# A fused four-layer network: cross attention of the last layer in two passes through DRAM, and layer 0 with its turned copies a step earlier

## The chip, the cores and the metric

The kernel runs on one core of a Trainium2 chip. The metric is the device time of one execution in microseconds (us), the median of several runs. The engines are TensorE (PE in the rows), VectorE (DVE), ScalarE (ACT), GpSimd (POOL) and the queue engine SyncE (SP), which issues nearly all DMA transfers. TensorE's clock has two levels, 1.2 and 2.4 GHz; the column PEclk of a stretch is the granted share of the full clock.

## The reference, cut to what matters

Four layers run one after the other on x of 8 entries x 100 tokens x 512: a grouped cross attention (32 heads over 8 key heads, layer 0), an RWKV layer, a plain attention, and layer 3, which has two cross attentions and an MLP. Context has 8 x 361 x 512 values. Layer 3 is (16 heads of 128, queries 100 tokens, keys and values 361 rows and one learned row):

```python
def _cross_attention(q_in, kv_in, wq, bq, wk, bk, wv, bv, wo, bo, bias_k, bias_v):
    qh = (q_in @ wq + bq).reshape(b, q_len, H, K)
    kh = (kv_in @ wk + bk).reshape(b, t, H, K)
    vh = (kv_in @ wv + bv).reshape(b, t, H, K)
    kh = jnp.concatenate([kh, jnp.broadcast_to(bias_k, (b, 1, H, K))], axis=1)
    vh = jnp.concatenate([vh, jnp.broadcast_to(bias_v, (b, 1, H, K))], axis=1)
    logits = jnp.einsum('bqhk,bthk->bhqt', qh, kh) / scale
    weights = jax.nn.softmax(logits, axis=-1)
    ctx = jnp.einsum('bhqt,bthk->bqhk', weights, vh).reshape(b, q_len, H * K)
    return ctx @ wo + bo
...
    h = _layer_norm(x, ln1_scale, ln1_offset)
    x = res + _cross_attention(h, xf_1, wq1, bq1, wk1, bk1, wv1, bv1, wo1, bo1, bias_k1, bias_v1)
    ...
    x = res + _cross_attention(h, xf_2, wq2, bq2, wk2, bk2, wv2, bv2, wo2, bo2, bias_k2, bias_v2)
```

## The kernel before

X stays in SBUF from layer to layer. Each layer opens a scope, in it a block with one program for each engine, ordered by hand and joined by semaphores. Matmuls of layer 3 take each operand as a high and a low part and use three products (low x high, high x low, high x high), the helper `products`.

**Layer 3.** `attention_block` (L2127) starts the first loads, runs the layer norm with its turning (highT, lowT), and calls `cross_attention` (L1469), twice in all. That runs 32 steps: 4 groups of 4 heads, for each the 8 entries. The engines' loops are hardware loops over half groups (4 steps). One step of TensorE (L1884) makes the keys of the entry for the 4 heads (48 matmuls, 362 wide), turns the probabilities of the step before (12 transposes), makes values (36 matmuls, 512 wide) with the attended product of the step before between them, the output product of the step before (12 matmuls, 512 wide), and the scores of this step (12 matmuls, 362 wide). Each fourth step starts with the queries of a half (48 matmuls, 400 wide). ScalarE copies high parts out of the banks (keys L1689, turned probabilities L1664, values L1699, attended L1669 and L1672) and makes the exponentials (L1657); VectorE makes the low parts, maxima and the normalising. POOL splits each loaded context into high and low (L1595, L1597) and each of the four weights of a group (L1610, L1612), each one when TensorE has let go of the buffer. VectorE adds each step's output to X. SP loads contexts and weights ahead.

**Layer 0.** `grouped_attention` (L190) runs 25 tiles for each of the 8 entries. In step n TensorE makes score n in one of RS banks (L562), and turns tile n-LT in one of RT banks (L519); it waits for the copy that frees the bank. VectorE adds the mask and takes the maximum (L476) and turns some copies out; ScalarE's step n is the exponential of tile n (L408) and then the copy of turned tile n-LE (L398).

## Time and profile before

| what | us |
|---|---|
| median of 3 runs (range) | 3397.99 (3397.32 to 3402.0) |
| profiled execution, its time | 3401.78 |
| profiled execution, its span | 3400.0 |
| load and start of layer 0 | 0 to 78 |
| layer 0, attention | 78 to 391 |
| rest of layer 0, layers 1 and 2 | 391 to 1280.6 |
| layer 3, first attention block | 1280.6 to 2247.9 |
| layer 3, second attention block | 2247.9 to 3215.6 |
| MLP and end | 3215.6 to 3400 |

Over the span TensorE is busy 2887.7 us (85%), VectorE 1613.1, ScalarE 980.1 and GpSimd 879.9. A matmul's duration overlaps the next one's, so the time that one costs TensorE is the distance from its start to the next start. A time in brackets at the end of a row is how long the engine stood idle before it, with the instruction that ended it.

### The profile page before, as it was taken

The numbers are of one execution on the slowest core, as the hardware profiler recorded it, in microseconds if no ns is written. First come the engines' busy times: TensorE is split into PE (matmuls) and PEld (weight loads), VectorE is DVE, ScalarE is ACT, GpSimd is POOL, SyncE is SP. The second block draws the span as 40 slices with busy tenths as digits, with TensorE's granted clock in tenths as the row PEclk, the third lists the DMA queues.
The fourth block names the chain that finished last, engine by engine and source line by source line (L and its number), as shares of the span: only waits on it lengthen the run. The fifth ranks groups of instructions, "written<-read, shape, count | busy, mean of one in ns | idle before, by whom it ended". The sixth has DMA issues, their size and how long they took to land. (4 is left out here: it accounts for less than half of the span.)

```text
span 3400.0 us, 42583 instructions
## 1 busy us (share of the span) xinstructions
PE 2887.7 (85%) x14746; PEld 2274.8 (67%) x14746; DVE 1613.1 (47%) x2985; ACT 980.1 (29%) x2236; POOL 879.9 (26%) x465
## 2 busy tenths in 40 slices
PE   5777749766678796998998999959989989989789
PEld 3555324333333465987987988948878879879689
DVE  2444451099952126445445445455454454454453
ACT  1555311100021113333333333333333323323231
POOL 2000022145510005333343342132352343432020
PEclk8888768899989997999999999969999999999889
DMA  4343010310000323111111101011111111100110
GB/s 151 79 94 91 11 61 39 119 37 20 20 0 0 118 72 113 39 39 51 39 51 39 39 30 35 10 70 61 39 55 35 39 56 46 39 17 26 53 50 20
DMA packets 73361, 170.13 MB, mean 50 GB/s; under 512 B 12180, under 2 KB 28972, under 8 KB 72236
## 3 DMA queue, kind: packets, MB, share of 16 engines
q1 hardware_dynamic: 73196, 168.77, 15.6%
q8 instruction: 57, 0.93, 0.1%
q14 instruction: 44, 0.36, 0.0%
q10 hardware_dynamic: 64, 0.07, 0.0%
HBM read 152.52 MB, written 14.65 MB: 49 GB/s over the span
## 5 line engine op out<-in xcount | busy, mean ns | idle before, releaser
L1595 POOL TENSOR_TENSOR ca_ch<-att_craw,ca_nothing 128x1448 fp32r<-128x1448 f32 x64 | 167.1, 2611 | 843.1 <-PE ca_ring L1821 843.0
L1821 PE MATMUL ca_ring<-ca_ch,ca_wl 128*128 128x362 f32 x1024 | 343.0, 335 | 26.1 <-DVE ca_ql L1777 26.1
L1821 PE MATMUL ca_ring<-ca_ch,ca_wh 128*128 128x362 f32 x1024 | 342.1, 334 | 0.0
L1821 PE MATMUL ca_ring<-ca_cl,ca_wh 128*128 128x362 f32 x1024 | 341.6, 334 | 0.0
L1657 ACT ACTIVATE ca_probs<-ca_score,ca_shift 100x362 f32<-100x362 f32 x256 | 140.7, 563 | 335.8 <-DVE ca_shift L1802 335.8
L1784 DVE SCALAR_TENSOR_TENSOR ca_kl<-ca_ring,ca_columns,ca_kh 128x361 fp32r<-128x361 f32 x256 | 145.7, 590 | 171.1 <-ACT ca_kh L1689 171.1
L1821 PEld LDWEIGHTS ca_ring<-ca_ch,ca_wl 128*128 128x128 f32 x1024 | 197.8, 193 | 28.8 <-DVE ca_ql L1777 16.8
L1597 POOL TENSOR_TENSOR ca_cl<-att_craw,ca_ch 128x1448 fp32r<-128x1448 f32 x64 | 215.6, 3369 | 5.0
L1689 ACT ACTIVATE ca_kh<-ca_ring,ca_columns 128x361 fp32r<-128x361 f32 x256 | 143.7, 567 | 254.0 <-PE ca_ring L1821 253.7
L1821 PE MATMUL ca_ring<-ca_wh,ca_cl 128*128 128x512 f32 (+1 forms) x512 | 205.4, 401 | 0.0
L1821 PE MATMUL ca_ring<-ca_wh,ca_ch 128*128 128x512 f32 (+1 forms) x512 | 201.7, 394 | 0.0
L1821 PE MATMUL ca_ring<-ca_wl,ca_ch 128*128 128x512 f32 (+1 forms) x512 | 201.3, 393 | 0.0
L1821 PEld LDWEIGHTS ca_ring<-ca_cl,ca_wh 128*128 128x128 f32 x1024 | 197.9, 193 | 0.0
L1821 PEld LDWEIGHTS ca_ring<-ca_ch,ca_wh 128*128 128x128 f32 x1024 | 197.2, 193 | 0.0
L871 PE MATMUL rec_sum<-rec_seen,l_gather 128*128 128x400 f32 x256 | 122.7, 563 | 85.9 <-POOL rec_seen L885 85.9
L476 DVE CUSTOM_DVE_ANT_0 ga_masked<-ga_score,ga_maskb 128x361 f32<-128x361 f32 x200 | 105.7, 534 | 161.2 <-PE ga_score L562 144.6
L1758 DVE TENSOR_TENSOR ca_mid<-ca_mid,ca_ring 128x200 f32<-128x200 f32 x64 | 23.3, 363 | 326.4 <-ACT ca_mid L1669 326.4
L909 DVE TENSOR_TENSOR_SCAN rec_state<-rec_wb,rec_rank 128x400 f32<-128x400 f32 x128 | 177.7, 1393 | 0.0
L1745 DVE TENSOR_SCALAR ca_probs<-ca_probs,ca_share 100x362 f32<-100x362 f32 x256 | 175.6, 749 | 2.3
L519 PE MATMUL ga_turn<-state_ident,ga_probs 128*128 128x128 f32 x600 | 118.7, 314 | 66.6 <-ACT ga_probs L408 50.8
L885 POOL TENSOR_TENSOR rec_seen<-rec_state,rec_rb 128x400 f32<-128x400 f32 x128 | 138.5, 1085 | 137.4 <-DVE rec_state L909 135.3
L1610 POOL TENSOR_TENSOR ca_wh<-att_raw,ca_nothing 128x2048 fp32r<-128x2048 f32 x24 | 86.5, 3602 | 286.6 <-PE ca_ring L1821 286.6
(355 smaller groups left out, 6797.5 us busy)
## 6 DMA issues: line engine op xcount, KB each, us to landing
att_craw<-in_ctxT SPq DMA_DIRECT2D x64, 724.0 KB
att_raw<-in_L_xattn_wq SPq DMA_DIRECT2D x8, 1024.0 KB
att_raw<-in_L_xattn_wk SPq DMA_DIRECT2D x8, 1024.0 KB
att_raw<-in_L_xattn_wv SPq DMA_DIRECT2D x8, 1024.0 KB
att_raw<-in_L_xattn_wo SPq DMA_DIRECT2D x8, 1024.0 KB
mlp_raw<-in_L_xattn_w_fc SPq DMA_DIRECT2D x4, 2048.0 KB
l_ctx<-in_ctxT SPq DMA_DIRECT2D x8, 724.0 KB
l2a_ctxT<-in_ctxT SPq DMA_DIRECT2D x8, 724.0 KB, 4.8
```

The costliest lines, as they stand in the source:

```text
L476: nc.vector.tensor_tensor_reduce(masked[:, n % RM, :], score[n % RS][:, 0:S], maskb[:, b % 2, lb, :], -1.0, 3.0e38, ALU.add, ALU.min, top[ ...
L519: last = nc.tensor.transpose(turn[n % RT][:, t, :], probs[:, n % RP, t * P:(t + 1) * P], ident[:])
L871: nc.tensor.matmul(sumb[par][:, :, 0:L], gather[:, j, :], seen[j % 4][:].rearrange("p (c l) -> p c l", l=L), start=(j == 0), stop=(j == HD ...
L885: nc.gpsimd.tensor_tensor(seen[j % 4][:], state[j % 4][:], rb[:, par].rearrange("p c l -> p (c l)"), ALU.mult).then_inc(seen_done, 1)
L909: nc.vector.tensor_tensor_scan(state[j % 4][:], wb[:, par].rearrange("p c l -> p (c l)"), rank1[:, j].rearrange("p c l -> p (c l)"), 0.0, ...
L1595: nc.gpsimd.tensor_tensor(flat(ch[:, parity]), flat(craw[:]), nothing[:].broadcast_to([P, CC * SP]), ALU.add).then_inc(ctx_high, 1)
L1597: nc.gpsimd.tensor_tensor(cl[:, parity], craw[:], ch[:, parity].bitcast(F32), ALU.subtract).then_inc(ctx_ready, 1)
L1657: nc.scalar.activation(probs[:, h, :], score[h][0:L, 0:SP], ACT.Exp, bias=shift[:, h:h + 1], scale=scale, accum_out=total[:, h:h + 1]).the ...
L1689: nc.scalar.activation(kh[:, h, 0:S], ring[h][:, 0:S], ACT.Identity, bias=column(1, n, h)).then_inc(high_done, 1 if i or h < G3 - 1 else 1 ...
L1745: nc.vector.tensor_scalar(probs[:, h, :], probs[:, h, :], share[:, h:h + 1], None, ALU.mult).then_inc(probs_ready, 1)
L1784: nc.vector.scalar_tensor_tensor(kl[:, h, 0:S], ring[h][:, 0:S], column(1, n, h), kh[:, h, 0:S].bitcast(F32), ALU.add, ALU.subtract).then_ ...
L1821: last = nc.tensor.matmul(out, a, b, start=(k == 0), stop=(k == count - 1))
```

## The change

**Layer 3** is split in two passes. `projections` (L1469 of the changed kernel) splits all 8 contexts once and keeps them in SBUF, makes all queries (32 units of 12 matmuls, 400 wide) and then all keys (128 units of 12 matmuls, 362 wide), and writes them to DRAM: queries as high and low parts (13.1 MB), keys as whole numbers (23.7 MB); X with the output bias is written there too. `attention` (L1681) reads them back a step ahead. A key comes into `kl`; ScalarE copies its high part to `kh` (`high_key`), POOL subtracts in place (`low_key`). Values are no longer made: the turned probabilities are multiplied with the raw context (`mix`, 36 matmuls, 400 wide), which POOL splits for each step, and each fourth step the value weights (`heads`, 4 x 13 matmuls, 400 wide, with one matmul for the learned row, whose probabilities SP gathers with three small transfers a step, `stack_extra`) and the output weights (`outputs`, 48 matmuls, 400 wide) are applied to half a group. The output is summed turned, in `acc`, and turned back and added to X at the end of the block, after X was read back: X's room serves as the landing place of contexts and weights meanwhile. All loops are unrolled.

**Layer 0**: `RS` 4 to 3, `RT` 2 to 3, one lag of 5 for the turning and its copy, and ScalarE's copy now stands ahead of the exponential in a step. The load of X waits for a small memset.

ScalarE, a middle step of the block, before: four exponentials of a step, then the first key copies out of the banks (probs: probabilities; kh: key's high part).

```order
L1657 ACTIVATE ca1_probs,ca1_total<-ca1_score0,ca1_shift 100x362
L1657 ACTIVATE ca1_probs,ca1_total<-ca1_score1,ca1_shift 100x362
L1657 ACTIVATE ca1_probs,ca1_total<-ca1_score2,ca1_shift 100x362
L1657 ACTIVATE ca1_probs,ca1_total<-ca1_score3,ca1_shift 100x362
L1688 ISA
L1689 ISA
L1689 ACTIVATE ca1_kh<-ca1_ring0,ca1_columns 128x361
L1688 REGISTER_ALU
L1689 ISA
L1689 ACTIVATE ca1_kh<-ca1_ring1,ca1_columns 128x361
```

The same engine after, one whole step n of the attention pass (pp: turned probabilities of n; yh: mixed context of n; probs: of n+2; kh: key of n+3).

```order
L1909 ACTIVATE ca1_pp<-ca1_ring0 128x400
L1909 ACTIVATE ca1_pp<-ca1_ring1 128x400
L1909 ACTIVATE ca1_pp<-ca1_ring2 106x400
L1915 ACTIVATE ca1_yh<-ca1_ring3 128x4x100
L1900 ACTIVATE ca1_probs,ca1_total<-ca1_score0,ca1_shift 100x362
L1915 ACTIVATE ca1_yh<-ca1_ring0 128x4x100
L1900 ACTIVATE ca1_probs,ca1_total<-ca1_score1,ca1_shift 100x362
L1915 ACTIVATE ca1_yh<-ca1_ring1 128x4x100
L1900 ACTIVATE ca1_probs,ca1_total<-ca1_score2,ca1_shift 100x362
L1915 ACTIVATE ca1_yh<-ca1_ring2 128x4x100
L1900 ACTIVATE ca1_probs,ca1_total<-ca1_score3,ca1_shift 100x362
L1894 ACTIVATE ca1_kh<-ca1_kl 128x1448
```

The key copy is now one of 1448 columns, and stands behind the last copy of the mixed context.

POOL in the block, before: two contexts and one weight.

```order
L1595 TENSOR_TENSOR ca1_ch<-att1_craw,ca1_nothing 128x1448
L1597 TENSOR_TENSOR ca1_cl<-att1_craw,ca1_ch 128x1448
L1608 ISA
L1609 ISA x2
L1610 TENSOR_TENSOR ca1_wh<-att1_raw,ca1_nothing 128x2048
L1611 ISA
L1612 TENSOR_TENSOR ca1_wl<-att1_raw,ca1_wh 128x2048
```

POOL after, steps 0 to 2 of the attention pass (kl: a key's low part; xh, xl: a context's parts; wvh, wvl: the value weights' parts; state_X is the landing place).

```order
L1854 TENSOR_TENSOR ca1_kl<-ca1_kl,ca1_kh 128x1448
L1861 TENSOR_TENSOR ca1_xh<-state_X,ca1_nothing 128x1536
L1864 TENSOR_TENSOR ca1_xl<-state_X,ca1_xh 128x1536
L1854 TENSOR_TENSOR ca1_kl<-ca1_kl,ca1_kh 128x1448
L1861 TENSOR_TENSOR ca1_xh<-state_X,ca1_nothing 128x1536
L1864 TENSOR_TENSOR ca1_xl<-state_X,ca1_xh 128x1536
L1870 TENSOR_TENSOR ca1_wvh<-state_X,ca1_nothing 128x2048
L1872 TENSOR_TENSOR ca1_wvl<-state_X,ca1_wvh 128x2048
L1854 TENSOR_TENSOR ca1_kl<-ca1_kl,ca1_kh 128x1448
```

A key's subtraction was added ahead of each context's two, and the weights' stand between.

ScalarE at the start of layer 0's attention, before (ga_turn0, 1: the banks of turned tiles).

```order
L395 ACTIVATE ga_kh<-ga_front,l0_bk 128x362
L408 ACTIVATE ga_probs<-ga_masked,ga_top 128x361 x7
L398 ACTIVATE ga_lturned<-ga_turn0 128x384
L408 ACTIVATE ga_probs<-ga_masked,ga_top 128x361
L398 ACTIVATE ga_turned<-ga_turn1 128x3x128
```

And after:

```order
L395 ACTIVATE ga_kh<-ga_front,l0_bk 128x362
L410 ACTIVATE ga_probs<-ga_masked,ga_top 128x361 x5
L398 ACTIVATE ga_lturned<-ga_turn0 128x384
L410 ACTIVATE ga_probs<-ga_masked,ga_top 128x361
L398 ACTIVATE ga_turned<-ga_turn1 128x3x128
L410 ACTIVATE ga_probs<-ga_masked,ga_top 128x361
L398 ACTIVATE ga_turned<-ga_turn2 128x3x128
```

The first copy stands two exponentials earlier, and copies go through three banks.

The diff, cut:

```diff
-    RS, RM, RP, RT = 4, 6, 6, 2
-    LT, LE = 5, 6
+    RS, RM, RP, RT = 3, 6, 6, 3
+    LAG = 5
...
-            for n in range(total + LE):
+            for n in range(total + LAG):
                 b, i = place(n)
+                if n >= LAG and not by_dve(n - LAG):
+                    keep_turned(act, n - LAG, copy, kept_act)
                 if n < total:
                     act.wait_ge(masked_done, n + 1)
                     if n >= RP:
                         act.wait_ge(turn_full, n - RP + 1)
                     nc.scalar.activation(probs[:, n % RP, 0:S], masked[:, n % RM, :], ACT.Exp, bias=top[:, n % RM:n % RM + 1],
                                          scale=-1.0).then_inc(exp_done, 1)
-                if n >= LE and not by_dve(n - LE):
-                    keep_turned(act, n - LE, copy, kept_act)
...
-                if LT <= n < total + LT:
-                    turn_tile(n - LT)
+                if LAG <= n < total + LAG:
+                    turn_tile(n - LAG)
...
+    BANKS = 8
+    QS, KS = 2, 4
...
+            for k in range(2 * NG3):
+                g, half = k // 2, k % 2
+                sp.wait_ge(query_low, G3 * (k + 1))
+                sp.dma_start(queries[g, :, :, :, half * HALF:(half + 1) * HALF], qstage[:, k % QS].bitcast(F32)).then_inc(
+                    queries_out[k % QS], 16)
+                if k + 2 < B:
+                    load_context(k + 2)
+                if half == 1:
+                    load_weights(g + 2)
+            for n in range(STEPS):
+                sp.wait_ge(kept_act, G3 // 2 * (n + 1))
+                sp.wait_ge(kept_dve, G3 // 2 * (n + 1))
+                sp.wait_ge(learned, n + 1)
+                sp.dma_start(keys[n], kstage[:, n % KS]).then_inc(keys_out[n % KS], 16)
...
+            for b in range(B):
+                split_context(b)
...
+            for g in range(NG3):
+                pe.wait_ge(weight_ready, g + 1)
+                for half in range(2):
+                    rows = slice(half * BH, (half + 1) * BH)
+                    for h in range(G3):
+                        bank_free(u - BANKS)
+                        products(nc, bank[u % BANKS][:, 0:HALF].rearrange("p (b l) -> p b l", l=L), [
+                            (weight(g, h, c), (highT[:, rows, c, :], lowT[:, rows, c, :])) for c in range(CC)]).then_inc(full, 1)
+                        u += 1
+            for n in range(STEPS):
+                g, b = n // B, n % B
+                j = NG3 + g
+                pe.wait_ge(weight_ready, j + 1)
+                if g == 0:
+                    pe.wait_ge(ctx_ready, b + 1)
+                for h in range(G3):
+                    bank_free(u - BANKS)
+                    products(nc, bank[u % BANKS][:, 0:SP], [
+                        (weight(j, h, c), (ch[:, b, c, :], cl[:, b, c, :])) for c in range(CC)]).then_inc(full, 1)
+                    u += 1
...
+        raw, craw = spare[:, 0:CC * W3], spare[:, CC * W3:CC * W3 + 3 * C].rearrange("p (t c) -> p t c", c=C)
+        acc = sc.sb("acc", [P, CC, B * L])
...
+            def load_key(n):
+                if n >= 2:
+                    sp.wait_ge(score_full, G3 * (n - 1))
+                sp.dma_start(kl[:, n % 2], keys[n]).then_inc(k_in[n % 2], 16)
...
+            def load_context(n):
+                sp.wait_ge(x_ready, n)
+                b = n % B
...
+            def stack_extra(n):
+                sp.wait_ge(turn_low, 3 * (n + 1))
...
+                if n + 2 < STEPS:
+                    load_query(n + 2)
+                    load_key(n + 2)
+                if n + 1 < STEPS:
+                    load_context(n + 1)
+                if n % B == 0:
+                    load_differences(n // B)
+                if n % B == 2:
+                    load_outputs(n // B)
+                if n % B == B - 2 and n + 2 < STEPS:
+                    load_values(n // B + 1)
+                stack_extra(n)
...
+            def low_key(n):
+                pool.wait_ge(k_high, n + 1)
+                nc.gpsimd.tensor_tensor(kl[:, n % 2].bitcast(F32R), kl[:, n % 2], kh[:, n % 2].bitcast(F32), ALU.subtract).then_inc(k_ready, 1)
...
+            low_key(0)
+            low_key(1)
+            split_context(0)
+            for n in range(STEPS):
+                if n + 2 < STEPS:
+                    low_key(n + 2)
+                if n + 1 < STEPS:
+                    split_context(n + 1)
+                g = n // B
+                if n % B == 1:
+                    split_weights(wvh, wvl, wv_ready, o_full, g, 2 * g + 1)
+                if n % B == 3:
+                    split_weights(woh, wol, wo_ready, out_full, g, 2 * g + 2)
...
+            def high_key(n):
+                act.wait_ge(k_in[n % 2], 16 * (n // 2 + 1))
+                if n >= 2:
+                    act.wait_ge(score_full, G3 * (n - 1))
+                nc.scalar.activation(kh[:, n % 2], kl[:, n % 2], ACT.Copy).then_inc(k_high, 1)
...
+            for n in range(-2, STEPS + 1):
+                if 0 <= n < STEPS:
+                    for t in range(3):
+                        turned_high(n, t)
+                j = half_due(n)
+                if j is not None:
+                    for h in range(G3):
+                        head_high(j, h)
+                for k in range(G3):
+                    if 0 <= n < STEPS:
+                        mixed_high(n, k)
+                    if n + 2 < STEPS:
+                        exponential(n + 2, k)
+                if n >= -1 and n + 3 < STEPS:
+                    high_key(n + 3)
...
+            def scores(n):
+                pe.wait_ge(q_in[n % 2], 16 * (n // 2 + 1))
+                pe.wait_ge(k_ready, n + 1)
...
+            def mix(n):
+                pe.wait_ge(x_ready, n + 1)
+                pe.wait_ge(turn_low, 3 * (n + 1))
+                for c in range(CC):
+                    bank_free(pe, "y", n, c)
+                    part = slice(c * P, (c + 1) * P)
+                    products(nc, bank_of("y", n, c)[:, 0:G3 * L], [
+                        ((xh[0:rows, n % 2, t, part], xl[0:rows, n % 2, t, part]), (pp[0:rows, t, 0, :], pp[0:rows, t, 1, :]))
+                        for t, (_, rows) in enumerate(STILES)]).then_inc(y_full, 1)
+            def heads(j):
+                pe.wait_ge(wv_ready, j // 2 + 1)
+                pe.wait_ge(vdiff_in, 48 * (j // 2 + 1))
+                pe.wait_ge(extra_in, 48 * BH * (j + 1))
+                pe.wait_ge(y_low, CC * BH * (j + 1))
                 for h in range(G3):
+                    bank_free(pe, "o", j, h)
+                    out = bank_of("o", j, h)[:, 0:HALF]
+                    nc.tensor.matmul(out, vdiff[:, h * K3:(h + 1) * K3], extra[:, h].rearrange("p b l -> p (b l)"), start=True, stop=False)
+                    products(nc, out, [
+                        ((wvh[:, c * W3 + h * K3:c * W3 + (h + 1) * K3], wvl[:, c * W3 + h * K3:c * W3 + (h + 1) * K3]),
+                         (yh[:, c, h].rearrange("p b l -> p (b l)"), yl[:, c, h].rearrange("p b l -> p (b l)")))
+                        for c in range(CC)], first=False).then_inc(o_full, 1)
+            def outputs(j):
+                pe.wait_ge(wo_ready, j // 2 + 1)
+                pe.wait_ge(o_low, G3 * (j + 1))
+                for c in range(CC):
+                    bank_free(pe, "out", j, c)
+                    products(nc, bank_of("out", j, c)[:, 0:HALF], [
+                        ((woh[:, h * C + c * P:h * C + (c + 1) * P], wol[:, h * C + c * P:h * C + (c + 1) * P]),
+                         (oh[:, h, :], ol[:, h, :])) for h in range(G3)]).then_inc(out_full, 1)
...
+            for n in range(-2, STEPS + 1):
+                if 0 <= n < STEPS:
+                    turn(n)
+                if n + 2 < STEPS:
+                    scores(n + 2)
+                j = half_due(n)
+                if j is not None:
+                    heads(j)
+                if 0 <= n < STEPS:
+                    mix(n)
+                if j is not None:
+                    outputs(j)
+            turn_rows(0)
+            turn_rows(1)
...
+            nc.vector.memset(spare[P - 32:P, CC * W3 + 2 * C:CC * W3 + 3 * C], 0.0).then_inc(cleared, 1)
+            sp.wait_ge(cleared, 1)
+            sp.dma_start(X, x_dram.rearrange("b l c -> l b c")).then_inc(come, 16)
```

## Rows read from the trace of the kernel before

**Rows 1.** Windows: from:to, length, busy us of each engine, granted clock, DMA share, GB/s

```profile
78.00:391.00 313.00, 242.21 (x1772) 159.56 (x1775) 148.83 (x494) 176.40 (x359) 11.62 (x19) 0.86 0.34 84
1280.60:2247.90 967.30, 896.24 (x5024) 803.10 (x5024) 470.58 (x853) 330.09 (x805) 313.88 (x113) 0.95 0.13 42
2247.90:3215.60 967.70, 895.65 (x5024) 802.09 (x5024) 470.39 (x853) 330.08 (x805) 314.08 (x113) 0.95 0.13 42
1341.00:1573.00 232.00, 228.84 (x1309) 205.94 (x1308) 109.50 (x210) 83.52 (x207) 76.32 (x26) 0.99 0.13 44
```

**Rows 2.** Timeline, TensorE, one step of block 1: start, duration, line, out<-in, count, idle before

```profile
1855.62 0.39 PE L1821 MATMUL ca_ring<-ca_wh,ca_ol 128*100 128x512 f32 x1
...
1858.38 0.33 PE L1821 MATMUL ca_score<-ca_kh,ca_ql 128*100 128x362 f32 x1
...
1868.34 1.19 PE L1845 MATMUL ca_ring<-state_ident,ca_probs 100*128 100x100 f32 x12
1869.31 0.48 PE L1821 MATMUL ca_score<-ca_wh,ca_cl 128*128 128x512 f32 x1
```

**Rows 3.** Timeline, TensorE, around the queries of the second group's second half

```profile
1535.66 0.34 PE L1821 MATMUL ca_ring<-att_lowT,ca_wh 128*128 x1
...
1537.49 0.34 PE L1821 MATMUL ca_ring<-att_highT,ca_wh 128*128 x1
1540.34 0.43 PE L1821 MATMUL ca_ring<-ca_ch,ca_wl 128*128 128x362 f32 x1 [2.51 <-DVE ca_ql L1777]
...
1541.61 0.46 PE L1821 MATMUL ca_ring<-ca_cl,ca_wh 128*128 128x362 f32 x1
...
1542.16 0.50 PE L1821 MATMUL ca_ring<-ca_ch,ca_wl 128*128 128x362 f32 x1
...
1544.58 0.50 PE L1821 MATMUL ca_ring<-ca_ch,ca_wh 128*128 128x362 f32 x1
...
1545.14 0.33 PE L1821 MATMUL ca_ring<-ca_cl,ca_wh 128*128 128x362 f32 x1
```

**Rows 4.** Timeline, ScalarE, in the step of rows 2

```profile
1862.46 0.56 ACT L1657 ACTIVATE ca_probs<-ca_score,ca_shift 100x362 f32<-100x362 f32 x1
...
1869.09 1.28 ACT L1664 ACTIVATE ca_pp<-ca_ring 128x400 fp32r<-128x400 f32 x3
```

**Rows 5.** Groups by line and form: count | busy us, mean ns of one | idle before

```profile
L1595 POOL TENSOR_TENSOR ca_ch<-att_craw,ca_nothing 128x1448 fp32r<-128x1448 f32 x64 | 167.1, 2611 | 843.1 <-PE ca_ring L1821 843.0
L1597 POOL TENSOR_TENSOR ca_cl<-att_craw,ca_ch 128x1448 fp32r<-128x1448 f32 x64 | 215.6, 3369 | 5.0
L1612 POOL TENSOR_TENSOR ca_wl<-att_raw,ca_wh 128x2048 fp32r<-128x2048 f32 x24 | 110.1, 4586 | 1.9
L1610 POOL TENSOR_TENSOR ca_wh<-att_raw,ca_nothing 128x2048 fp32r<-128x2048 f32 x24 | 86.5, 3602 | 286.6 <-PE ca_ring L1821 286.6
L1647 ACT ACTIVATE ca_wh<-att_raw 128x2048 fp32r<-128x2048 f32 x8 | 15.1, 1908 | 2.9 <-PEq L35 2.9
```

**Rows 6.** Timeline, start of block 1: VectorE, POOL and the first matmul

```profile
1304.53 2.97 DVE L1723 TENSOR_TENSOR ca_wl<-att_raw,ca_wh 128x2048 fp32r<-128x2048 f32 x1 [1.84 <-ACT ca_wh L1647]
1305.44 5.19 POOL L1597 TENSOR_TENSOR ca_cl<-att_craw,ca_ch 128x1448 fp32r<-128x1448 f32 x1
...
1307.56 0.70 PE L1821 MATMUL ca_ring<-att_highT,ca_wl 128*128 128x400 f32 x1 [7.92 <-DVE ca_wl L1723]
```

**Rows 7.** DMA issues of layer 2: out<-in, count, KB each, us from issue to landing

```profile
l2a_ctxN<-in_ctx SPq DMA_DIRECT2D x8, 512.0 KB, 5.7
```

**Rows 8.** Layer 0: TensorE's turning as a group of the page, then a timeline

```profile
L519 PE MATMUL ga_turn<-state_ident,ga_probs 128*128 128x128 f32 x600 | 118.7, 314 | 66.6 <-ACT ga_probs L408 50.8
```

**Rows 9.** Timeline of layer 0, all engines, two tiles

```profile
256.59 0.41 PE L562 MATMUL ga_score<-ga_ks,ga_qs 96*128 96x362 f32 x1
...
257.61 0.60 ACT L408 ACTIVATE ga_probs<-ga_masked,ga_top 128x361 f32<-128x361 f32 x1 [1.26 <-DVE ga_top L476]
...
258.12 0.47 ACT L398 ACTIVATE ga_turned<-ga_turn 128x384 f32<-128x384 f32 x1
...
258.69 0.52 PE L519 MATMUL ga_turn<-state_ident,ga_probs 128*128 128x128 f32 x3 [1.19 <-ACT ga_probs L408]
...
258.96 0.41 PE L562 MATMUL ga_score<-ga_ks,ga_qs 96*128 96x362 f32 x1
```

799 lines of the change are left out of this document (414 added, 385 removed).

## The prediction, written before the run

> **What bounds the kernel now.** I read the windows first, by stage [rows 1]. The two attention blocks of layer 3 take 967.3 and 967.7 us of the 3400, and TensorE is busy for 896 of each; in the eight steps from 1341 to 1573 it is busy for 228.84 of 232, so a step of 29.0 us is TensorE's own work. Layer 0's attention is different: 242.21 busy of 313, at a granted clock of 0.86. There the page puts 50.8 of TensorE's 66.6 idle us down to ScalarE [rows 8].
>
> **Layer 3, TensorE's work.** A matmul costs its distance to the next start. Twelve 512-wide take 2.76 us from 1855.62 to 1858.38 [rows 2], 0.23 each; ten 400-wide take 1.83 from 1535.66 to 1537.49 [rows 3], 0.183; twelve transposes 0.97 [rows 2]. Of 362-wide ones, eight in 2.42 us at the lower clock, from 1542.16 to 1544.58, are 0.302 each [rows 3]; at the full clock 0.166, by their width against the 400-wide ones. Before, a step has 48 keys (8.0), 36 values (8.3), the output (2.8), scores (2.0), transposes (1.0), a quarter of 48 queries (2.2) and the 24 narrow attended products, about 27 in all. After, keys 8.0, queries 2.2, transposes 1.0, scores 2.0, 36 mixed (6.6), a quarter of 52 heads (2.4) and of 48 outputs (2.2): 24.4. By TensorE's work alone a block would lose 2.6 x 32 = 83 us. Whether it does depends on what stands between.
>
> **First pass.** Until the first query 27 us, as now (the block starts at 1280.6, its first matmul at 1307.56 [rows 6]); queries 384 x 0.183 = 70; two cold microseconds; keys 1536 x 0.166 = 255. Eight banks cover the copies, and a step's keys leave in 8.0 us through four buffers; a transfer of 512 KB lands in 5.7 [rows 7], so 724 KB ought to in about 8. POOL splits a context in 2.61 + 3.37 = 6.0 us [rows 5]; eight take 48 and fit beside the 100 us before the keys, but SP's loads of contexts and weights wait for each other's landing place, and I set 8 for all such waits and 8 for draining the stores and opening the next pass. Sum: 27 + 73 + 8 + 255 + 8 = 371.
>
> **Second pass, the chain.** The order rows of ScalarE show the key copy of step n+3 behind the last mixed copy and the last exponential of step n. POOL's subtraction of the same key follows it, then TensorE's scores of n+3, and in TensorE's order the mix of n+1 stands behind these. So nothing overlaps along this circle:
> - mix 36 x 0.183 = 6.6;
> - the last mixed copy 0.43 (three 400-wide in 1.28 [rows 4]) and 0.1 for the hand-over;
> - the last exponential 0.56 [rows 4];
> - the key copy, 1448 columns: between 0.43 for 400 and 1.91 for 2048 [rows 5] lies 1.4;
> - POOL's subtraction of 128x1448, the form of L1597: 3.37 [rows 5];
> - hand-over 0.15, scores 2.0.
>
> That is 14.6 us, for 6.6 + 2.0 + 1.0 = 9.6 of TensorE's work. The key has two buffers, but they don't help, since the copy's place in ScalarE's program holds it back. TensorE then idles 5.0 us less hand-overs in each such step, with only the transposes in the gap. VectorE (maxima, normalising, low parts) works inside it. In the step whose scores are followed by the heads the circle gets 52 x 0.183 = 9.5 more: 24.1. In the one after it, the outputs (8.8) stand between mix and scores and hide the chain: 6.6 + 8.8 + 1.0 + 2.0 = 18.4. Between the 32 steps there are 31 distances: 15 x 14.6 + 7 x 24.1 + 7 x 18.4 + 2 x 11 at the end, where no key is left to fetch, = 539. POOL also splits eight weights between, 3.60 + 4.59 = 8.2 each [rows 5]. A step of POOL is 3.4 + 6.3 (context of 1536 columns, by the two rows of 1448), and with a weight 17.9 against 14.6: 8 x 3.3 = 26. Filling (two keys and a context through POOL before the first mix, after a landing) 31; the tail (mix 6.6, heads 9.5, outputs 8.8, their copies 3, turning back and adding 6) 34. Pass: 31 + 539 + 26 + 34 = 630. Block: 1001, that is +34 on 967.
>
> **What the new gaps do to the clock.** Behind a gap of 2.51 us TensorE falls to the lower of its levels from 1541.61 to 1545.14 [rows 3]: 11 matmuls at 0.302 instead of 0.166, 1.5 us. After the change 22 distances of a block have a gap of twice that length. 22 x 1.5 = 33 a block; if the rest of the clock's fall grows with the gap, up to twice as much. So +67 a block, +134 for both.
>
> **Transfers.** A step now brings 724 KB of key, 400 of queries and 722 of context, 1.9 MB in 14.6 us, and SP issues the next key behind the three small `stack_extra` transfers, which wait for the low turned parts, that is for the start of mix n. The key then has some 8 us until ScalarE wants it; 5.7 us for 512 KB [rows 7] puts it at the limit. Taken at nothing; if each key came 2 us late it would be 22 x 2 x 2 = 88 more. POOL has 9.7 of 14.6 us to do, so the context is on time.
>
> **Layer 0.** In the two-tile circle score (256.59), exponential (257.61), copy (258.12), turn (258.69), score (258.96) [rows 9] 2.37 us pass. Turn m waits for copy m-2, which stands behind exponential m+4, which needs score m+4. With three banks, and the copy ahead of the exponential, turn m waits for copy m-3, behind exponential m+1: three tiles of slack, and the circle is gone. Next is TensorE's own work. The 50.8 us [rows 8] go, and with fewer gaps part of 242 x 0.14 = 34 us of lost clock comes back; the score's bank, now three, can cost a little. Stacking the keys in DRAM between entries may set a floor. Bounds 20 and 85; I take 60, near the wait that the row names. The load order at the start: one or two us, nothing against these.
>
> **Sum.** 3400.0 + 134 - 60 = 3474 of span, and the profiled execution, 3401.78, becomes 3476. It lies 3.8 above the median, so the median goes from 3398 to **3471**.
>
> **A rule of the skill.** In rows 6 a POOL subtraction beside VectorE's two-input one of 2.97 us took 5.19, where the mean of its form is 3.37 [rows 5]. The Trainium skill, "GPSIMD Engine Reference", section 1 (Specifications), says that POOL's SBUF interfaces are shared with VectorE, with contention where VectorE has two SBUF inputs; the row agrees. By the mean the circle is 14.6, by that one row 16.4, and rival C is made of it.
>
> **Rivals.**
> - **A, the other side: layer 0 gives more than the blocks lose.** TensorE keeps 2.4 GHz through gaps of 5 us and layer 0 gives its whole 85: 2 x 34 - 85 = -17, 3381. It decides at a point: faster once layer 0's gain exceeds both blocks' loss. For it: the block's loss of 34 hangs on fill, tail and weights, some 90 us guessed to a third. Against: both the gap in rows 3 and layer 0's 0.86 show a lower clock where TensorE waits. 0.14.
> - **B, TensorE's work bounds the second pass after all**, because the key copies run ahead. 2 x -83 - 60, with fill and tail back at 2 x 20: about 3210. The order rows speak against it. 0.03.
> - **C, the chain is longer.** The subtraction at 5.19: 1.8 x 22 x 2 = +80, 3551; or late keys, +88, 3559; or the clock stays low through most of the second pass (36 + 12 matmuls at nearly double, 5 us in each of 62 distances, beyond 3700). For it: VectorE works in just this gap, with two-input subtractions and normalising. Against: late in the block the form holds its mean. 0.19.
> - **D, losses and gains meet** within 7 us of 3398: 0.06.
> - My forecast, 3405 to 3535: 0.58.
>
> **How the numbers follow.** About 0.2% (7 us) is what a measurement of this kernel can tell from no change. Faster: A and B, 0.17; same: D, 0.06; slower: forecast and C, 0.77. The range has to leave out at most 0.2: B, the lower half of A, and the upper part of C, above 3590. It is 3380 to 3590.
>
> **What would show it.** In the changed trace, right: scores waiting for POOL's key subtraction in most steps, a distance of 14.6 to 16.5 between mixes, and TensorE busy about two thirds of the second pass at a clock below 0.95; the first pass with TensorE over 90% busy and about 370 us long; layer 0 near 253 us with no wait of the turning for ScalarE. Wrong: steps of 10 us (B), ScalarE's key copy waiting for a DMA (late keys), subtractions of 5 us (C), layer 0 above 290.

## The result, and the profile after

The changed kernel takes 3553.99 us (median of 4 runs, 3544.54 to 3566.45) against 3398.64 (3397.32 to 3402.0): a ratio of 1.0458, 95% interval 1.0424 to 1.0491. The forecast was slower and 3471; it is slower by 155 us, about twice the 73 that I had summed. The time lies in the upper part of the range.

Windows of the changed kernel (columns as in [rows 1]): block 1, block 2; then, within block 1, the first pass, the opening of the second pass, and the distance from the first mix to the last.

```profile
1213.80:2291.40 1077.60, 855.64 (x4704) 834.26 (x4704) 496.94 (x767) 319.55 (x676) 447.00 (x180) 0.88 0.34 116
2291.40:3373.90 1082.50, 855.41 (x4704) 834.17 (x4704) 494.18 (x766) 319.32 (x676) 446.61 (x180) 0.87 0.34 116
...
1239.00:1576.00 337.00, 330.81 (x1920) 329.47 (x1920) 74.61 (x103) 66.83 (x103) 61.93 (x55) 0.98 0.39 145
1576.00:1622.00 46.00, 13.27 (x47) 11.50 (x48) 11.42 (x24) 11.16 (x23) 21.05 (x10) 0.57 0.61 189
1622.00:2252.00 630.00, 472.51 (x2539) 457.65 (x2537) 379.67 (x576) 224.01 (x514) 350.81 (x106) 0.85 0.30 100
```

Against [rows 1] the two blocks grew by 110 and 115 us, though TensorE is busy for 40 us less in each. Layer 3 starts at 1213.8 instead of 1280.6, 67 us earlier, and what follows it is 5 us shorter: 110 + 115 - 67 - 5 = 153, the difference of the two spans (3552.8 and 3400.0). The first pass is what it was taken for. The loss sits in the 630 us, where TensorE works for 472 at a granted clock of 0.85.

What TensorE waited for (us in total, times, longest), the changed kernel:

```profile
PE ca_ring L2033 <- DVE ca_probs L1966: 229.8, 50, 14.2
PE ca_score L1464 <- issue: 92.0, 30, 3.8
```

The profile names no releaser in the second line ("issue"); the timelines of the plain step below show that it is the chain I had forecast, since the scores start 0.10 us behind the end of POOL's subtraction. The first line is not the forecast's: the turning of probabilities (L2033) waits for VectorE's normalising (L1966), up to 14 us at a time. The groups of the page, with the turning of layer 0 that answers to [rows 8]:

```profile
L1966 DVE TENSOR_SCALAR ca_probs<-ca_probs,ca_share 100x362 f32<-100x362 f32 x256 | 285.9, 1119 | 0.1
L519 PE MATMUL ga_turn<-state_ident,ga_probs 128*128 128x128 f32 x600 | 106.8, 290 | 1.7 <-issue 1.0 <-DVE ga_turned L273 0.3
```

Idle time before layer 0's turning fell from 66.6 us to 1.7. Over the whole stage (78 to 324 for 78 to 391) TensorE is idle for 37.3 us instead of 70.8, and busy for 208.7 instead of 242.2 at a granted clock of 0.93 instead of 0.86. So only half of the 67 us is idle time; the other half goes with the clock. New idle time stands at the starts of the entries: 28.0 us in seven places before the first score (L557), for 9.2 in one. A normalising takes 1119 ns in the mean; its median in this trace is 401 ns and its longest 10170.

**A plain step.** Timelines of the changed kernel; the rows of TensorE, then ScalarE's key copy and POOL's subtraction in the same step:

```profile
1751.11 1.25 PE L2033 MATMUL ca_ring<-state_ident,ca_probs 100*128 100x100 f32 x12 [1.52 <-DVE ca_probs L1966]
1755.39 0.59 PE L1464 MATMUL ca_score<-ca_kh,ca_q 128*100 128x362 f32 x1 [3.04 <-issue]
...
1759.10 0.54 PE L1464 MATMUL ca_ring<-ca_pp,ca_xl 128*128 128x400 f32 x1
```

```profile
1750.56 1.41 ACT L1894 ACTIVATE ca_kh<-ca_kl 128x1448 fp32r<-128x1448 f32 x1
...
1752.05 3.24 POOL L1854 TENSOR_TENSOR ca_kl<-ca_kl,ca_kh 128x1448 fp32r<-128x1448 f32 x1 [6.28 <-ACT ca_kh L1894]
```

The copy of 1.41 us starts behind the last exponential, the subtraction of 3.24 ends at 1755.29, and the scores start at 1755.39. Twelve of them take 3.71 us, to 1759.10, where 2.05 is what they take at the full clock behind a half's outputs. The granted clock is 0.50 from 1755.39 to 1759.10. From mix to mix 16.1 us pass in the mean; the forecast was 14.6 for the circle and 1.5 for the clock.

**A weight step.** POOL and VectorE in the step in which an output weight is split:

```profile
2014.47 3.60 POOL L1870 TENSOR_TENSOR ca_woh<-state_X,ca_nothing 128x2048 fp32r<-128x2048 f32 x1
2018.14 4.54 POOL L1872 TENSOR_TENSOR ca_wol<-state_X,ca_woh 128x2048 fp32r<-128x2048 f32 x1
2022.65 3.33 POOL L1854 TENSOR_TENSOR ca_kl<-ca_kl,ca_kh 128x1448 fp32r<-128x1448 f32 x1
2025.94 2.84 POOL L1861 TENSOR_TENSOR ca_xh<-state_X,ca_nothing 128x1536 fp32r<-128x1536 f32 x1
```

```profile
2015.00 3.27 DVE L1966 TENSOR_SCALAR ca_probs<-ca_probs,ca_share 100x362 f32<-100x362 f32 x1
2018.19 0.56 DVE L1977 TENSOR_TENSOR ca_yl<-ca_ring,ca_yh 128x400 fp32r<-128x400 f32 x1
2018.68 4.22 DVE L1966 TENSOR_SCALAR ca_probs<-ca_probs,ca_share 100x362 f32<-100x362 f32 x1
2022.82 0.56 DVE L1977 TENSOR_TENSOR ca_yl<-ca_ring,ca_yh 128x400 fp32r<-128x400 f32 x1
2023.30 2.89 DVE L1966 TENSOR_SCALAR ca_probs<-ca_probs,ca_share 100x362 f32<-100x362 f32 x1
2026.11 0.56 DVE L1977 TENSOR_TENSOR ca_yl<-ca_ring,ca_yh 128x400 fp32r<-128x400 f32 x1
2026.59 2.40 DVE L1966 TENSOR_SCALAR ca_probs<-ca_probs,ca_share 100x362 f32<-100x362 f32 x1
```

```profile
2029.05 2.26 PE L2033 MATMUL ca_ring<-state_ident,ca_probs 100*128 100x100 f32 x12 [10.24 <-DVE ca_probs L1966]
```

Each normalising of 0.4 us ends 0.2 us behind the end of a POOL instruction: 2018.27 behind 2018.07, 2022.90 behind 2022.68, 2026.19 behind 2025.98, 2028.99 behind 2028.78. I call this wait the hold. Over the whole trace, each of the 65 normalisings that started with more than 0.6 us of a POOL instruction left took at least 2.03 us and ended 0.20 or 0.21 us behind the end of a POOL instruction; none of the 191 beside which POOL rested took more than 0.41. The subtractions between them (L1977), one operand of which is in PSUM, are not held. In a plain step POOL rests while VectorE normalises; with 8.1 us of weight in the way POOL runs without a break through all four. The Trainium skill, "SBUF — State Buffer", section "Who interferes with whom", says that a VectorE instruction in a two-port mode (it names tensor_scalar among those that can enter one) and a GpSimd instruction share a pair of ports by an exclusive lock that is kept for the whole instruction, whoever comes first. The trace agrees, with the ends above; that the normalising runs in such a mode no row says. The same section says that a VectorE instruction with one operand from SBUF and no such mode is free of it, as the 0.56 us of L1977 show.

### The profile page after: what moved, and what is told of

Same layout as the page of the kernel before. It is cut to its first block and busy times, and to the rows that moved or that the text cites. A ratio compares the mean times of both kernels' runs of the same rounds, so it can differ in the third digit from the quotient of the medians.

```text
span 3552.8 us, 38907 instructions
## 1 busy us (share of the span) xinstructions
PE 2773.7 (78%) x14106; PEld 2335.4 (66%) x14106; DVE 1659.8 (47%) x2812; ACT 952.0 (27%) x1976; POOL 1145.2 (32%) x599
## 5 line engine op out<-in xcount | busy, mean ns | idle before, releaser
L1464 PE MATMUL ca_ring<-ca_pp,ca_xh 128*128 128x400 f32 (+1 forms) x1536 | 411.3, 349 | 0.0
L1854 POOL TENSOR_TENSOR ca_kl<-ca_kl,ca_kh 128x1448 fp32r<-128x1448 f32 x64 | 209.5, 3274 | 557.2 <-ACT ca_kh L1894 557.2
L1464 PE MATMUL qk_bank<-qk_ch,qk_wl 128*128 128x362 f32 x1024 | 337.4, 330 | 2.6 <-DVE qk_wl L1613 2.6
L1464 PE MATMUL qk_bank<-qk_ch,qk_wh 128*128 128x362 f32 x1024 | 336.2, 328 | 0.0
L1464 PE MATMUL qk_bank<-qk_cl,qk_wh 128*128 128x362 f32 x1024 | 335.9, 328 | 0.0
L1464 PE MATMUL ca_score<-ca_kh,ca_q 128*100 128x362 f32 x512 | 194.9, 452 | 147.8 <-issue 92.0
L1464 PEld LDWEIGHTS ca_ring<-ca_pp,ca_xh 128*128 128x128 f32 (+1 forms) x1536 | 293.8, 195 | 0.3
L1966 DVE TENSOR_SCALAR ca_probs<-ca_probs,ca_share 100x362 f32<-100x362 f32 x256 | 285.9, 1119 | 0.1
L2033 PE MATMUL ca_ring<-state_ident,ca_probs 100*128 100x100 f32 (+1 forms) x768 | 98.9, 291 | 229.8 <-DVE ca_probs L1966 229.8
L1464 PE MATMUL ca_ring<-ca_pp,ca_xl 128*128 128x400 f32 (+1 forms) x768 | 272.2, 354 | 5.6 <-issue 3.1
L2033 PEld LDWEIGHTS ca_ring<-state_ident,ca_probs 100*128 100x128 f32 (+1 forms) x768 | 85.5, 163 | 247.2 <-DVE ca_probs L1966 246.7
L1864 POOL TENSOR_TENSOR ca_xl<-state_X,ca_xh 128x1536 fp32r<-128x1536 f32 x64 | 225.8, 3527 | 5.0
L1977 DVE TENSOR_TENSOR ca_yl<-ca_ring,ca_yh 128x400 fp32r<-128x400 f32 x256 | 145.8, 570 | 156.3 <-ACT ca_yh L1915 156.3
L1464 PEld LDWEIGHTS qk_bank<-qk_cl,qk_wh 128*128 128x128 f32 x1024 | 194.1, 190 | 0.0
```

What stands on the lines that cost most here:

```text
L1464: issued = nc.tensor.matmul(out, x, y, start=(first and k == 0), stop=(last and k == count - 1))
L1854: nc.gpsimd.tensor_tensor(kl[:, n % 2].bitcast(F32R), kl[:, n % 2], kh[:, n % 2].bitcast(F32), ALU.subtract).then_inc(k_ready, 1)
L1864: nc.gpsimd.tensor_tensor(xl[:, n % 2], craw, xh[:, n % 2].bitcast(F32), ALU.subtract).then_inc(x_ready, 1)
L1966: nc.vector.tensor_scalar(probs[:, n % 2, h, :], probs[:, n % 2, h, :], share[:, n % 2, h:h + 1], None, ALU.mult).then_inc(probs_done, 1)
L1977: nc.vector.tensor_tensor(yl[:, c, :, n % BH, :], bank_of("y", n, c)[:, 0:G3 * L].rearrange("p (h l) -> p h l", l=L), yh[:, c, :, n % BH, ...
L2033: last = nc.tensor.transpose(bank_of("turn", n, t)[0:rows, h * L:(h + 1) * L], probs[:, n % 2, h, s0:s0 + rows], ident[0:L, 0:L])
```

## The experiments

The distances below are between the first matmuls of one mix and the next, read from TensorE's timeline of block 1 of each kernel. Steps 1, 9, 17, 25 split a value weight; 3, 11, 19, 27 an output weight, and the heads come in the same distance.

| kernel | median us | ratio to before | plain | value weight | into a half | output weight | first to last mix |
|---|---|---|---|---|---|---|---|
| changed | 3554 | 1.046 | 16.1 | 23.3 | 26.4 | 31.2 | 629.8 |
| e2 weights off POOL | 3482 | 1.0245 | 16.7 | 16.3 | 27.2 | 27.2 | 592.7 |
| e3 key early | 3512 | 1.033 | 13.1 | 23.3 | 23.9 | 34.2 | 605.2 |
| e4 normalising on ScalarE | 3484 | 1.0247 | 16.8 | 17.6 | 26.6 | 27.2 | 596.3 |
| e11 weights in quarters | 3503 | 1.030 | 16.4 | 18.1 | 27.3 | 29.3 | 606.5 |
| e5 three together | 3229 | 0.951 | 11.4 | 10.1 | 20.8 | 24.0 | 472.1 |
| e6 keys in parts | 3431 | 1.011 | 11.7 | 20.4 | 22.0 | 34.9 | 570.4 |
| e7 parts, normalising | 3218 | 0.947 | 12.1 | 11.1 | 21.2 | 19.4 | 465.9 |
| e9 loads ahead | 3160 | 0.929 | 10.4 | 9.8 | 19.1 | 19.2 | 434.4 |
| e8 filled gaps | 3592 | 1.057 | 14.8 | 26.7 | 24.2 | 40.0 | 657.4 |
| e10 e4 and filled gaps | 3479 | 1.023 | 16.7 | 16.3 | 26.4 | 26.2 | 585.9 |
| e12 and the shift | 3445 | 1.014 | 15.6 | 15.7 | 25.0 | 27.2 | 571.5 |

"Plain" is the mean of the distances that hold nothing but a step (without the first and the last two), the other columns are means of four or three. Behind a half's outputs the distance is 18.2 or 18.3 in all of them; 18.4 was forecast.

### Layer 0 alone

```diff
 # the kernel before
-    RS, RM, RP, RT = 4, 6, 6, 2
-    LT, LE = 5, 6
+    RS, RM, RP, RT = 3, 6, 6, 3
+    LAG = 5
...
+                if n >= LAG and not by_dve(n - LAG):
+                    keep_turned(act, n - LAG, copy, kept_act)
                 if n < total:
```

> The kernel before with the change of layer 0 alone (three banks for turned tiles, three for scores, ScalarE's copy ahead of the exponential). In the changed kernel layer 3 starts at 1213.8 us instead of 1280.6. If all of that is layer 0's attention, this kernel takes 3398 - 67 = 3331 us and its two attention blocks stay at 967 us each. If part of the 67 us came from the changed order of the first loads, which is not in this kernel, it takes 3335 to 3345.

3330.9 us, ratio 0.9797 (0.9778 to 0.9815). Layer 0 is worth 67 us alone, the load order nothing that shows in a spread of 3325 to 3336, and the blocks are unchanged (967.6 us from 1213.8 to 2181.4). The wait that the row of [rows 8] names is gone, but it is not the whole account: by the figures above, half of it came back as idle time before the scores, and the clock gave as much again.

### Weights off POOL

```diff
 # the changed kernel, ScalarE and VectorE of attention
+                    if n % B == 1:
+                        round_weights(wvh, o_full, g, 2 * g + 1)
+                    if n % B == 3:
+                        round_weights(woh, out_full, g, 2 * g + 2)
...
+                nc.vector.tensor_tensor(low[:], raw, high[:].bitcast(F32), ALU.subtract).then_inc(ready, 1)
```

> The changed kernel, with the value and output weights of the attention pass split by ScalarE (high) and VectorE (low) instead of POOL. Theory of the hold (VectorE's normalising waits for the end of whatever POOL instruction runs, and with a weight's two instructions POOL runs without a break): the eight weight steps of a block lose their extra 8.4 and 5.0 us, 54 a block, and pay 1 to 3 us each for VectorE's own low part: about 3554 - 108 + 32 = 3478 us. Theory of the queue (the weights only delay the key's subtraction behind them, 3.3 us each): 26 a block, 3502 us or more.

3482.1 us (1.0225 to 1.0265): the hold's 3478, not the queue's 3502. Both weight distances are now as long as those without a weight.

### The normalising on ScalarE

```diff
-                nc.vector.tensor_scalar(probs[:, n % 2, h, :], probs[:, n % 2, h, :], share[:, n % 2, h:h + 1], None,
-                                        ALU.mult).then_inc(probs_done, 1)
+                nc.scalar.activation(probs[:, n % 2, h, :], probs[:, n % 2, h, :], ACT.Copy,
+                                     scale=share[:, n % 2, h:h + 1]).then_inc(probs_done, 1)
```

> The changed kernel, with the normalising of the probabilities on ScalarE instead of VectorE; nothing else is moved. Theory of the hold: the weight steps lose what lies above POOL's queue, 54 - 26 = 28 a block, and ScalarE's last normalising lengthens the circle by 0.5 us in 44 distances (22 us): about 3520 us. Theory of the queue: the weight steps stay as long, 3576 us.

3483.9 us (1.0226 to 1.0269), better than the 3520 of the hold's theory. POOL does the same work in the same order here, so what is left in the weight distances is the price of its queue: 4 x (17.6 - 16.8) + 4 x (27.2 - 26.6) = 5.6 us a block, of 48 in the changed kernel. The distance of 17.6 is POOL's own work in such a step (by the durations in the changed kernel, 3.24 + 2.74 + 3.54 + 3.60 + 4.54 = 17.7). I had 26 for the eight in the expectation and in the prediction.

### Weights in quarters

```diff
+                for c in range(CC):
+                    part = slice(c * W3, (c + 1) * W3)
+                    nc.gpsimd.tensor_tensor(high[:, part], raw[:, part], nothing[:].broadcast_to([P, W3]), ALU.add).then_inc(
+                        weight_high, 1)
```

> The changed kernel, with each of POOL's two instructions for a weight cut into four of 512 columns, in the same place and queue. Theory of the hold (a normalising of VectorE waits for the end of the POOL instruction that runs): it is now held for about 1 us instead of 3 to 4 in these steps, and the 48 extra us of a block's weight steps fall to 10 to 20: 3554 - 2 x 33 = 3490 us. Theory of the queue (POOL's total work is late): the work is the same or longer, 3554 us or more.

3502.7 us. The weight distances fell from 23.3 and 31.2 to 18.1 and 29.3, a block's extra from 48 to 15: within the 10 to 20, with POOL's work the same and only the length of its instructions changed. The total gained 51 where 64 was expected; the distances into a half grew by 0.9, and why is open.

### The key early

```diff
                     for t in range(3):
                         turned_high(n, t)
+                    if n + 3 < STEPS:
+                        high_key(n + 3)
...
-                if n >= -1 and n + 3 < STEPS:
-                    high_key(n + 3)
```

> The changed kernel, with ScalarE's key copy of step n+3 moved ahead of the mixed copies of step n (behind the turned tiles), and the key's load one step earlier. Theory of the chain alone: the circle of 16.4 us is cut and TensorE's 9.6 us bound 44 distances, 3554 - 299 = 3255 us. Chain and hold: POOL now has 9.6 us of work in a step and never rests, so each of four normalisings is held to the end of a POOL instruction of about 3.2 us, a step takes about 13 us, and the kernel 3554 - 44 x 3.4 = 3404 us. If late transfers or the clock set the step and not the copy's place, nothing changes: 3554 us.

3512.3 us, where 3404 was expected with the hold and 3255 without. The chain was real: in the distances with no hold 11.3 us are left of 16.1. But POOL now stands in VectorE's way in other steps too; the normalising's mean rose to 1414 ns, and TensorE's wait for it from 229.8 to 296.7 us. One normalising missed a boundary between two POOL instructions (they end at 1684.35 and 1687.90) and waited through both:

```profile
1681.56 6.55 DVE L1971 TENSOR_SCALAR ca_probs<-ca_probs,ca_share 100x362 f32<-100x362 f32 x1
```

I had priced a hold at one instruction, 3.2 us.

### Three moves together

The weights off POOL and the early key as above, and the normalising on ScalarE ahead of the mixed copies (`invert` moved to the start of VectorE's step).

> The changed kernel with three moves together: weights split by ScalarE and VectorE instead of POOL, ScalarE's key copy a step earlier, and the normalising on ScalarE ahead of the mixed copies. Chain and hold together are the whole excess: with both gone TensorE (9.6 us a step) and POOL (9.6) bound, a plain step takes about 10.5 us instead of 16.4 and the distances of a pass sum to 446 instead of 630: 3554 - 368 = 3186 us. If something third (transfers, VectorE's low parts against POOL) holds the steps at 13 us as in the run with the early key alone, 3330 to 3400 us.

3228.5 us, 0.951 (0.949 to 0.953); 3186 expected. The excess is chain and hold: without both the kernel is faster than before. What was left over were scores waiting by one to three microseconds, 14 times in block 1 (26 us). This run also shows the contention from its other side. VectorE now makes the low parts of the weights, with both operands in SBUF, and where such an instruction started just ahead of POOL's, it was POOL that waited; ten POOL instructions took 5.4 to 5.7 us:

```profile
1778.18 2.29 DVE L1990 TENSOR_TENSOR ca_wol<-state_X,ca_woh 128x2048 fp32r<-128x2048 f32 x1
1778.22 5.67 POOL L1866 TENSOR_TENSOR ca_xl<-state_X,ca_xh 128x1536 fp32r<-128x1536 f32 x1
```

Without it a POOL instruction of this form takes 3.55 us.

### Keys in parts

```diff
-    keys = nc.dram_tensor(f"keys{i}", (STEPS, P, G3, SP), F32).ap()
+    keys = nc.dram_tensor(f"keys{i}", (STEPS, P, 2, G3, SP), F32).ap()
...
+                    nc.vector.scalar_tensor_tensor(kstage[:, n % KS, 1, h, 0:S], bank[(u + h) % BANKS][:, 0:S],
+                                                   column[:, g * G3 + h, 1:2], kstage[:, n % KS, 0, h, 0:S].bitcast(F32),
+                                                   ALU.add, ALU.subtract).then_inc(kept_dve, 1)
```

> The changed kernel with keys stored in DRAM as high and low parts by the first pass (ScalarE high, VectorE low, two stage buffers), so the second pass has neither ScalarE's key copy nor POOL's subtraction. Weights stay on POOL, the normalising on VectorE. Chain gone, hold only where POOL runs (6.3 us of a step, and the weight steps): plain steps 10.5 us, weight steps as long as they are: 3554 - 2 x 130 - 24 (shorter filling) = 3270 us. If transfers bound (2.6 MB a step), 13 us a step, 3400 us.

3431.2 us instead of 3270. The chain is gone with the instructions that made it (plain 11.7), and TensorE's wait for the normalising stays as it was:

```profile
PE ca_ring L2020 <- DVE ca_probs L1953: 229.7, 50, 14.3
```

The weight distances with the heads even grew, from 31.2 to 34.9. So cutting the chain alone leaves the hold as it is.

### Keys in parts and the normalising on ScalarE

> The kernel with keys in parts, and the normalising on ScalarE ahead of the mixed copies; POOL still splits contexts and weights. Theory: the hold is gone everywhere, TensorE bounds the second pass: 3554 - 2 x 184 - 24 = 3162 us, below both kernels and below 3331. If the transfers bound, as much as the run with keys in parts alone.

3218.1 us, 0.947 (0.945 to 0.949). The hold of the normalising is gone, but 3162 was missed by 56 us. Six of the ten plain distances are 10.5 to 11.2 us. In that trace a key's load was issued behind `stack_extra`, at 1706.27, and its scores started at 1713.62, 0.67 us late; 17 such waits sum to 31 us in block 1.

### The loads ahead

```diff
+                if n + 1 < STEPS:
+                    load_context(n + 1)
+                if n + 3 < STEPS:
+                    load_query(n + 3)
+                    load_key(n + 3)
...
                 stack_extra(n)
```

> The kernel with keys in parts and normalising on ScalarE (3218 us), with the query's and key's loads issued ahead of the three small transfers that wait for the turned parts, right when their buffer is free. In that kernel the scores waited some 1.4 us in most steps, 60 to 70 us in all, for keys issued 7 us before. If the place in SP's queue makes them late, these waits go: 3218 - 55 = 3163 us. If the transfers themselves are too slow for a step of 11 us, 3218 us stays.

3160.4 us, 0.929 (0.928 to 0.931), as expected, and the fastest kernel here: 238 us below the kernel before and 394 below the changed one. The same 434 us of block 1, the changed kernel and then this one:

```profile
1622.00:2056.00 434.00, 321.68 (x1726) 311.86 (x1725) 265.91 (x390) 154.14 (x353) 245.89 (x75) 0.85 0.31 104
```

```profile
1622.00:2056.00 434.00, 425.89 (x2538) 418.70 (x2536) 260.29 (x451) 238.67 (x605) 260.99 (x78) 0.99 0.57 195
```

TensorE is busy for 426 of 434 us at a granted clock of 0.99, and does in them all 31 distances; most plain ones take 9.8 or 9.9 us. 67 of the 238 us are layer 0's (e1). The idea of the change was sound in TensorE's own work (24.4 us a step against 27); what kept it back was the key's copy and subtraction in the second pass, the normalising on VectorE beside POOL's work, and the place of the loads in SP's queue.

### Filled gaps: the clock

```diff
+            def fill(n):
+                pe.wait_ge(exp_done, G3 * (n - 1) + 1)
+                for _ in range(16):
+                    nc.tensor.matmul(score[0][0:L, 0:P], ident[:, 0:L], ident[:], start=True, stop=True)
```

> The changed kernel with 16 idle matmuls (identity times identity, 128 wide, into a score bank that is free then) on TensorE in each gap of 3 us ahead of the scores; they add about 2.3 us of work inside the gap and nothing to the output. Theory of the clock: scores and the mixed products behind the gap run at the lower clock for 1.5 us a gap; with the gap filled they don't: 3554 - 44 x 1.5 = 3488 us. If the clock's fall comes from the other gap of 1.5 us or from the whole stretch's work, 3554 us or more.

The total went up to 3591.9, and the plain distances down, from 16.1 to 14.8. TensorE's timeline there: turning, the idle matmuls, scores, the next product.

```profile
1742.01 1.25 PE L2033 MATMUL ca_ring<-state_ident,ca_probs 100*128 100x100 f32 x12 [1.52 <-DVE ca_probs L1966]
1743.10 3.66 PE L2040 MATMUL ca_score<-state_ident 128*100 128x128 f32 x32
1746.52 0.41 PE L1464 MATMUL ca_score<-ca_kh,ca_q 128*100 128x362 f32 x1
```

The 16 idle matmuls are 32 in the trace and take 3.4 us, not 2.3, which just fills the gap; the scores behind them take 2.1 instead of 3.7, at a granted clock of 1.00 instead of 0.50. So in these steps the clock's price goes when the gap of 3 us is filled. In the weight steps there is no gap before the scores, the idle matmuls (4.4 and 5.2 us in the first two) are paid in full, and the wait for the normalising grew too (23.3 to 26.7 and 31.2 to 40.0).

> The kernel with normalising on ScalarE (3484 us, every distance plain, with a gap of 3.4 us before the scores), with the same 16 idle matmuls in each gap, which took 3.4 us in the run with filled gaps. In that run the plain distances fell from 16.2 to 14.8, but the weight steps, where there is no such gap, grew. Theory of the clock: here all 22 distances of a block fall by 1.4 to 1.6 us: 3484 - 44 x 1.5 = 3418 us. If the clock is not what the gap costs, 3484 us or more.

3478.9 us, against 3484 without the fill: a miss by 61. The granted clock of the whole run rose from 0.881 to 0.913 and the time hardly fell. VectorE's shift of the maxima is an instruction of the normalising's kind. It is held in the changed kernel too (median 1.72 us for 0.17), where the first exponential waits for it but the chain does not. In this kernel it was held as follows (minimum, median and longest, ns), and in 7 of the 21 distances of block 1 with idle matmuls the gap ahead of the turning grew from 1.6 us to between 2.3 and 3.1:

```profile
L1965 DVE TENSOR_SCALAR ca_shift<-ca_top x64: 170/1924/3547, 1607.5 to 3232.6; 100x4 f32<-100x4 f32 x64
```

> The kernel with filled gaps and normalising on ScalarE (3479 us), with the last small VectorE instruction of that form, the shift of the maxima (100x4), on ScalarE too. In that kernel it was held for up to 3.5 us (median 1.9, at least 0.17) while POOL split the context, and ScalarE waited for it, where the filled gap had brought it forward. Theory: the clock's 1.5 us a gap were gained and given back by this hold; now the 22 distances of a block fall from 16.7 to about 15.3: 3484 - 44 x 1.4 = 3422 us. If the fill's own 3.4 us are what eats the gain, 3479 us stays.

3444.9 us, 1.0143 (1.0126 to 1.016): 39 us of the 62 expected are there. Where a distance is 15.0 the whole gain shows; in five of the ten plain ones of block 1 it is 16.5. The trace tells what costs the other 1.5 us there. First a step of 16.5, then one of 15.0, turning and idle matmuls:

```profile
1722.94 1.25 PE L2034 MATMUL ca_ring<-state_ident,ca_probs 100*128 100x100 f32 x12 [1.62 <-ACT ca_probs L1908]
1724.03 5.33 PE L2041 MATMUL ca_score<-state_ident 128*100 128x128 f32 x32
1739.46 1.25 PE L2034 MATMUL ca_ring<-state_ident,ca_probs 100*128 100x100 f32 x12 [1.62 <-ACT ca_probs L1908]
1740.55 3.66 PE L2041 MATMUL ca_score<-state_ident 128*100 128x128 f32 x32
```

```profile
1724.03:1729.11 5.08, 5.08 (x35) 5.08 (x33) 1.54 (x3) 1.33 (x4) 4.85 (x2) 0.66 0.42 151
1740.55:1744.14 3.59, 3.59 (x34) 3.48 (x33) 1.53 (x3) 1.33 (x4) 3.36 (x2) 1.00 0.00 0
```

The idle matmuls themselves took 5.08 us instead of 3.59, at a granted clock of 0.66 instead of 1.00, and the scores stood behind them though POOL's subtraction had ended at 1727.51. The only gap over 0.1 us in the 35 us before was the one of 1.62 us ahead of the turning. So filling the gap of 3 us does not always keep the clock up, and the run with filled gaps, where it did in every plain step, had shown only one side of it. Why the clock fell in some steps and not in others, behind the same gap, stays open. In e10 the idle matmuls took 4.1 to 5.4 us in 14 of the 21 distances.

## Why the prediction was right or wrong

**The sign, and layer 0.** Slower was right, and for the larger part by the forecast's mechanism: the circle of ScalarE's key copy, POOL's subtraction, scores and mix, read from the order rows. Plain distances 16.1 for 14.6 + 1.5, behind a half 18.3 for 18.4, into a half 26.4 for 24.1 + 1.5. The durations taken from [rows 4, 5] held: key copy 1.41 for 1.4, subtraction 3.27 in the mean for 3.37. Layer 0 gave 67 for 60, as the sum of three: 65 less idle time before the turning (50.8 counted in the forecast), some 34 from the clock (of which the forecast took a part), and some 32 of other idle time added, mostly at the starts of the entries. The forecast had named a floor there, the stacking of the keys, without a price; the profile names no releaser for the new waits. That 60 was near is partly luck. First pass, to its last key: 361.5 for 363.

**The step that failed** is "A step of POOL is 3.4 + 6.3 ..., and with a weight 17.9 against 14.6: 8 x 3.3 = 26". The queue it describes costs 6 us a block (e4), for two reasons that its own numbers held: the distance to compare with is 14.6 and the clock's 1.5, and the four output weights stand in distances of 24.1, where 17.9 us of POOL's work fit. The weight steps cost 48, and 42 of them come by another way: VectorE's normalising waits for the end of POOL's instructions, which here follow each other without a break, and the turning and the next scores wait for the normalising. e2 takes the 48 away from POOL's side, e4 takes 42 from VectorE's, and e11 takes two thirds away by the length of POOL's instructions alone. I had the contention in the text, in the wrong direction: from the 5.19 us of [rows 6] I made a rival (C) in which POOL is slowed by VectorE. Its subtraction kept its 3.3 us (3.40 at the longest); VectorE was the one that waited. The other direction exists, as [rows 6] and e5 show, where VectorE has both operands in SBUF and starts first; in the changed kernel's attention pass no VectorE instruction with two SBUF operands stands there (the subtractions L1972 and L1977 take one from PSUM). The sentence "VectorE (maxima, normalising, low parts) works inside it" took for granted that its instructions keep their durations next to POOL.

**The other terms of a block**, forecast and measured:

| term | forecast | measured |
|---|---|---|
| first pass up to the last key | 363 | 361.5 |
| drain, opening and filling | 8 + 31 | 47.2 |
| distances without the weights' extra, clock included | 539 + 33 | 581.5 |
| weights' extra | 26 | 48.3 |
| last mix to the next stage | 34 | 39.0 |
| sum | 1034 | 1077.5 |

The two blocks are 43 and 48 us longer than forecast, 91 in all; layer 0 and the last stage give 12 of them back, which is the difference between 3474 and 3552.8 of span. The weights' extra is half of it (22); the rest is the opening and filling (8), the tail (5), and 9.5 in the distances: 5.5 into a half (26.4 for 25.6) and 5 in the last two (13.4 and 13.6 for 11). The plain ones are as forecast. What makes the filling and the tail longer was not tested; in the opening ScalarE's second key copy waits 2.6 us for its transfer. Two sums of the forecast are off by 1 us each, which changes nothing: queries and cold start are 70 + 2 = 72 and not 73, and 3476 less 3.8 is 3472.

**The rivals.** A did not come about: the clock fell in the gaps (0.85 over the second pass), and layer 0's 67 us alone were not enough. B, TensorE's own work as the bound, needed the key's chain, the hold and the loads' place gone (e9). C gave nearly the right time, 3551, for a reason that the trace refutes, so its number is luck; its other forms did not come about either. The mix ran at the full clock but for its first matmuls (0.97 from 1759.10 to 1767.54). Late keys cost little in the changed kernel: behind the opening ScalarE's key copy waited for its transfer four times in block 1, 0.8 to 1.5 us each. They were the next cause behind the two others: with steps of 11 us they showed, and e9 removed them.

## What to carry to other kernels

Before counting on work that hides in a gap, look whether the two engines that share the gap leave each other alone: here two short VectorE instructions from SBUF to SBUF (normalising and shift) took as long as whatever GpSimd instruction ran beside them. Removing one link of a circle alone paid 42 us of the 150 expected (e3, where the hold was priced in) and 123 of 284 (e6). In e3 the faster step put GpSimd's work over more of the normalisings; in e6 the hold stayed in the weight steps. The links had to go together. An instruction's place in its own engine's order sets a chain as much as its data do: from e4 to e5, where mainly the key copy and the normalising changed their places, the time fell by 255 us, and from e7 to e9, where only loads moved ahead of three small transfers, by 58; the matmuls saved were worth 166 by my sum.
